# Row maxima subtracted as three bf16 parts in one pass; units of the gated stage in pairs on different rows; new orders of work

## The reference

```python
x = ln(x + L0_attn(x));  x = ln(x + L0_xattn(x, ctx)); x = ln(x + L0_ffn(x))
x = ln(x + L1_attn(x));  x = ln(x + L1_xattn(x, ctx)); x = ln(x + L1_ffn(x))
x = ln(x + L2_attn(x));  x = ln(x + L2_xattn(x, ctx, ctx)); x = ln(x + L2_ffn(x))
x = ln(x + L3_attn(x));  x = ln(x + L3_xattn(x, ctx, ctx)); x = ln(x + L3_ffn(x))
# softmax layers: exp(s - max(s)) / sum(exp(s - max(s)))
# L3_xattn, 8 heads of 16 features:
cs = cumsum(log_sigmoid(f)); log_D = where(tril, cs[:, None] - cs[None, :] + i[None, :], -inf)
D = exp(log_D - max(log_D)); C = (q @ k.T / sqrt(16)) * D
h = C / (maximum(abs(sum(C)), exp(-max(log_D))) + 1e-6) @ v
```

## Time and profile before

| | us |
|---|---|
| median of 3 runs | 1140.05 |
| lowest, highest | 1136.43, 1142.04 |
| profiled execution | 1138.05 |
| its span, first to last instruction | 1136.2 |
| PE busy | 979.7 (86%) |
| VectorE busy | 570.7 (50%) |
| ScalarE busy | 414.3 (36%) |
| mean granted clock of PE | 0.891 |

### The profile page before, as it was taken

How to read it: one execution, slowest core, us unless ns; L and a number is a source line. 1 busy time by engine, 2 the same in 40 slices (tenths; PEclk the granted TensorE clock), 3 DMA queues, 4 the chain that set the end, 5 groups by cost and what they waited for, 6 DMA issues and landing times. The chain is left out here.

```text
span 1136.2 us, 20415 instructions
## 1 busy us (share of the span) xinstructions
PE 979.7 (86%) x8329; PEld 710.0 (62%) x8329; DVE 570.7 (50%) x1585; ACT 414.3 (36%) x873; POOL 44.5 (4%) x68
## 2 busy tenths in 40 slices
PE   7689898999899879988697979999989898898781
PEld 4237776788787846745245757868878685674431
DVE  5733567452464653634624853655346464534326
ACT  2035323243545725623024234234354463331211
POOL 1200000000100000000000000001010000000000
PEclk9699999899999979959659999989999989997755
DMA  9000003000003011110000000121000300000000
GB/s 335 10 1 2 1 1 149 2 34 1 17 1 126 1 37 39 62 73 1 1 10 1 1 1 2 56 94 34 1 17 1 126 1 1 1 1 1 1 0 19
DMA packets 6830, 35.97 MB, mean 32 GB/s; under 512 B 722, under 2 KB 4306, under 8 KB 5459
## 3 DMA queue, kind: packets, MB, share of 16 engines
q1 hardware_dynamic: 6738, 34.68, 8.2%
HBM read 34.15 MB, written 0.52 MB: 31 GB/s over the span
## 5 line engine op out<-in xcount | busy, mean ns | idle before, releaser
L641 PE MATMUL bank<-xT,weights_F 128*128 128x256 f32 x832 | 203.4, 390 | 0.7 <-ACT p L1766 0.6
L641 PEld LDWEIGHTS bank<-xT,weights_F 128*128 128x128 f32 x832 | 155.1, 196 | 21.7 <-issue 1.7
L649 PEld LDWEIGHTS bank<-weights_F,p 128*128 128x128 f32 x1088 | 134.4, 192 | 18.4 <-issue 6.5
L649 PE MATMUL bank<-weights_F,p 128*128 128x128 f32 x1088 | 140.5, 277 | 2.5 <-DVE p L1322 2.5
L1694 ACT ACTIVATE p<-bank 128x512 f32<-128x512 f32 x160 | 84.3, 602 | 137.8 <-PE bank L487 119.0
L1306 DVE SCALAR_TENSOR_TENSOR res<-bank,comb,res 128x128 f32<-128x128 f32 x184 | 55.8, 345 | 68.6 <-PE bank L649 65.1
L1322 DVE TENSOR_TENSOR p<-p,bank 128x512 f32<-128x512 f32 x72 | 49.4, 686 | 65.1 <-PE bank L641 33.1
L1147 DVE TENSOR_REDUCE m_wide<-bank 128x4 f32<-128x512 f32 x96 | 60.7, 683 | 39.3 <-PE bank L748 32.5
L1766 ACT ACTIVATE p<-bank 128x512 f32<-128x512 f32 x72 | 42.5, 597 | 96.8 <-PE bank L641 96.3
L1842 ACT ACTIVATE p<-bank 128x512 f32<-128x512 f32 x64 | 36.8, 598 | 58.4 <-PE bank L641 58.3
L513 PE MATMUL bank<-p,vz 128*32 128x128 f32 x1280 | 44.2, 286 | 9.4 <-ACT p L1694 8.8
(11 more groups left out here) (323 smaller groups left out, 1524.9 us busy)
## 6 DMA issues: line engine op xcount, KB each, us to landing
weights_F<-in_L1f SPq DMA_DIRECT2D x2, 4096.0 KB, 13.2
weights_F<-in_L0f SPq DMA_DIRECT2D x2, 3456.0 KB, 12.9
weights_F<-in_L2f SPq DMA_DIRECT2D x2, 3456.0 KB, 12.1
weights_Y<-in_L1x_kv SPq DMA_DIRECT2D x2, 1024.0 KB, 10.1
weights_Z<-in_L1x SPq DMA_DIRECT2D x2, 1024.0 KB, 11.1
weights_Y<-in_L2a SPq DMA_DIRECT2D x2, 898.0 KB, 4.4
weights_Z<-in_L2x SPq DMA_DIRECT2D x2, 449.0 KB, 3.2
weights_L3m<-in_L3m SPq DMA_DIRECT2D x2, 288.0 KB, 5.8
```

Of the source, the lines that this page charges most:

```text
L641: m = mm(b[:, k * NT:(k + 1) * NT], W[weight][:, f:f + P], s.xT[:], start=True, stop=True)
L649: m = mm(b[:, tk(u)], h[:, tk(u)], w, start=k == 0, stop=k == len(chunks) - 1)
```

## The change

Four edits.

- Maxima. After the reductions VectorE splits each set of maxima into three bf16 parts that add up to the f32 value: copy to bf16, subtract, copy the rest to bf16, subtract again (`split_maxima`, four operations of 128x16 that wait for each other, with a yield between). The parts lie in columns 4k to 4k+3 of each 32 of `m_wide`, `pick` takes rows 0 to 11 of each 32, `m_diag` and the ones are bf16. `turn_maxima` waits for the last of these operations, where it waited for the last reduction.
- L3x. Units go in pairs (0, 3) and (1, 2), whose products lie on rows 0 to 63 and 64 to 127 and whose row sums lie on rows 0 to 31 and 32 to 63 (32 rows each instead of 8). A pair opens two banks for the products and then two for the sums; the order is both pairs, retrieved(0), retrieved(1). VectorE and ScalarE follow.
- `v17` has memory of its own. Two constants are made at the start, and `WARM`, a table for extra matmuls, is there but empty.
- All strings of `TURN_ORDER` are new, those of POOL and SP too.

```diff
-    put("pick", -(p[:, None] % 32 == np.arange(4)).astype(np.float32))
+    put("pick", -((p[:, None] % 32 < 12) & (p[:, None] % 4 == np.arange(4))).astype(np.float32))
...
+WARM = {"a": "", "b": ""}
...
-            self.m_diag = own("m_diag", NS, 4, T)
+            self.m_diag = sb(f"m_diag_{g}", [P, NS, 4, T], BF16)
+            self.m_part = sb(f"m_part_{g}", [P, 2, H], BF16)
+            self.v17 = own("v17", NS, HC, DC + 1)
...
                 def turn_maxima(st, u):
                     b = opened("dve", st, "mT", u)
-                    if st == "L0x":
-                        pe.wait_ge(*told("maxima"))
-                    else:
-                        pe.wait_ge(*freed(st, "s", u, 0, 3))
+                    pe.wait_ge(*told("maxima"))
...
-                        m = mm(heads(b[:], 4), const("ones")[rows32(i), 0:T], s.m_diag[rows32(i), u], start=first, stop=not first)
+                        m = mm(heads(b[:], 4), ones_bf[rows32(i)], s.m_diag[rows32(i), u], start=first, stop=not first)
...
+                    def units(first, second):
+
+                        both = (first, second)
+                        banks = [opened("dve", "L3x", "s", i) for i in both]
+                        for i, b in zip(both, banks):
+                            u, half = i // 2, i % 2
+                            filled(mm(heads(b[:], 4), s.ctxT[rows64(half), tk(u)], s.bd_c[rows64(half), u], start=True, stop=True),
+                                   "L3x", "s", i)
+                        banks = [opened("act", "L3x", "D", i) for i in both]
+                        for b in banks:
+                            mm(heads(b[:], 4), ident_bf[:], among(neg_causal_t_bf[:], 4), start=True, stop=False)
+                        for i, b in zip(both, banks):
+                            u, half = i // 2, i % 2
+                            filled(mm(heads(b[:], 4), const("ones")[rows32(u), 0:T], s.m_diag8[rows32(u), 4 * half:4 * half + 4],
+                                      start=False, stop=True), "L3x", "D", i)
...
-                    unit(0)
-                    yield
-                    unit(1)
+                    units(0, 3)
+                    yield
+                    units(1, 2)
                     yield
                     pe.wait_ge(*told("L3x_v17"))
                     pe.wait_ge(*told("L3x_ones"))
                     retrieved(0)
                     yield
-                    unit(2)
-                    yield
-                    unit(3)
-                    yield
                     retrieved(1)
...
+                def split_maxima(u):
+
+                    part = lambda k: heads(s.m_wide[:, u], 4)[:, :, 4 * k:4 * k + 4]
+                    done = o.count(dve.tensor_copy(heads(s.m_part[:, 0], 4), part(0)))
+                    yield
+                    dve.wait_ge(*done)
+                    done = o.count(dve.tensor_tensor(part(1), part(0), heads(s.m_part[:, 0], 4), ALU.subtract))
+                    yield
+                    dve.wait_ge(*done)
+                    done = o.count(dve.tensor_copy(heads(s.m_part[:, 1], 4), part(1)))
+                    yield
+                    dve.wait_ge(*done)
+                    o.count(dve.tensor_tensor(part(2), part(1), heads(s.m_part[:, 1], 4), ALU.subtract), sem("maxima"))
...
+            dve.memset(zeros_bf[:], 0.0).then_inc(S("masks"), 1)
             take_turns("dve", program)
...
-                    for i in range(4):
+                    for i in (0, 3, 1, 2):
...
-                            sp.wait_ge(*ring.full((pair, "L3x", "s", 3)))
+                            sp.wait_ge(*ring.full((pair, "L3x", "s", 2)))
```

More of the change, by code:

```diff
@@ L146 @@
     "pe":
[10 rows of a table removed]
-    "dve":
[9 rows of a table removed]
-    "act":
[7 rows of a table removed]
[10 rows of a table added]
+    "dve":
[9 rows of a table added]
+    "act":
[7 rows of a table added]
     "pool":
-        "a1 b1 a2 b2 a2 b2 a1 b1 a4 b1 a1 b2 a1 b2 a1 b1 a2 b1 a4 b6 a3 b3 a4 b1 a1 b2 a1 b2 a1 b2 a3 b3 ",
+        "a1 b1 a1 b2 a3 b1 a1 b1 a1 b1 a2 b1 a2 b2 a1 b2 a1 b1 a2 b1 a4 b4 a1 b2 a2 b2 a1 b1 a2 b1 a2 b2 a1 b2 a1 "
+        "b1 a2 b1 a1 b3 ",
     "sp":
-        "a3 b3 a18 b18 a23 b23 ",
+        "a3 b6 a18 b12 a23 b26 ",
 }
+WARM = {"a": "", "b": ""}
 def build(nc, dram, out):
@@ L219, in _build @@
     neg_causal_t_bf = sb("neg_causal_t_bf", [P, P], BF16)
+    ones_bf = sb("ones_bf", [P, P], BF16)
+    zeros_bf = sb("zeros_bf", [P, P], BF16)
     ones_row = const("ones")[0:1, 0:128]
@@ L330, in __init__ @@
             self.m_diag8 = self.p[0:64, 4:6].rearrange("p a (h t) -> p (a h) t", h=4)
-            self.v17 = self.m_diag[:].rearrange("p u j t -> p (u j t)")[:, 0:NS * HC * (DC + 1)] \
-                .rearrange("p (u h d) -> p u h d", u=NS, h=HC)
         def apart(self, u, block=0):
@@ L409, in _, with warm @@
             mm, tr = pe.matmul, pe.transpose
+            def warm(b, n):
+                for _ in range(n):
+                    mm(heads(b[:], 4), ident_bf[:], among(zeros_bf[:], 4), start=True, stop=True)
             def program(g):
@@ L413, in program @@
                 key = pair = turn = None
+                warmth = iter(WARM["ab"[g]].split())
                 def opened(by, *a):
-                    return ring.open((pair, *a), by)
+                    b = ring.open((pair, *a), by)
+                    warm(b, int(next(warmth, 0)))
+                    return b
                 def filled(ins, *a):
@@ L995, in L3x @@
                     yield
-                    def unit(i):
-                        u, half = i // 2, i % 2
-                        b = opened("dve", "L3x", "s", i)
-                        mm(heads(b[:], 4), s.ctxT[rows64(half), tk(u)], s.bd_c[rows64(half), u], start=True, stop=True) \
-                            .then_inc(ring.filled((pair, "L3x", "s", i)), 1)
-                        b = opened("act", "L3x", "D", i)
-                        mm(heads(b[:], 4), ident_bf[:], among(neg_causal_t_bf[:], 4), start=True, stop=False)
-                        filled(mm(heads(b[:], 4), const("ones")[32 * u:32 * u + 8, 0:T],
-                                  s.m_diag8[32 * u:32 * u + 8, 4 * half:4 * half + 4], start=False, stop=True), "L3x", "D", i)
+                    def units(first, second):
[12 more added lines that the diff above has]
+                                      start=False, stop=True), "L3x", "D", i)
                     def retrieved(u):
@@ L1063, in _ @@
             pe.wait_ge(*weights("con"))
-            pe.wait_ge(S("masks"), 3)
+            pe.wait_ge(S("masks"), 5)
             take_turns("pe", program)
@@ L1148, in maxima @@
                                 free(st, "s", u, 0, i))
+                    yield
+                    dve.wait_ge(*freed(st, "s", u, 0, 3))
+                    yield from split_maxima(u)
                 def block_maxima(st, u, blk):
@@ L1159, in block_maxima @@
                             dve.wait_ge(free(st, "s", u, k, 3), ring.freed((pair, st, "s", u, k, 3))[1])
-                        o.count(dve.tensor_tensor(heads(s.m_wide[:, u], 4)[:, :, 0:4], heads(s.mx[:, u, 0], 4),
-                                                  heads(s.mx[:, u, 1], 4), ALU.max), sem("maxima"))
+                        done = o.count(dve.tensor_tensor(heads(s.m_wide[:, u], 4)[:, :, 0:4], heads(s.mx[:, u, 0], 4),
+                                                         heads(s.mx[:, u, 1], 4), ALU.max))
+                        yield
+                        dve.wait_ge(*done)
+                        yield from split_maxima(u)
                 def pick_maxima(st, u):
@@ L1564, in keep @@
                         return o.count(dve.tensor_copy(held[u][:, 0:HC * 17], b[:, 0:HC * 17]), free("L3x", "o", u))
-                    unit(0)
-                    yield
-                    unit(1)
-                    yield
+                    for i in (0, 3, 1):
+                        unit(i)
+                        yield
                     keep(0)
@@ L1624, in _ @@
             dve.wait_ge(*weights("con"))
-            for dst, src in ((ident_bf, IDENT), (neg_causal_bf, const("neg_causal")), (neg_causal_t_bf, const("neg_causal_t"))):
+            for dst, src in ((ident_bf, IDENT), (neg_causal_bf, const("neg_causal")), (neg_causal_t_bf, const("neg_causal_t")),
+                             (ones_bf, const("ones"))):
                 dve.tensor_copy(dst[:], src).then_inc(S("masks"), 1)
+            dve.memset(zeros_bf[:], 0.0).then_inc(S("masks"), 1)
             take_turns("dve", program)
```

## The result

| | us |
|---|---|
| before, median of 4 runs | 1139.72 (1136.43 to 1142.04) |
| changed, median of 4 runs | 1110.05 (1103.07 to 1114.31) |
| ratio | 0.9732, 95% interval 0.9699 to 0.9765 |
| profiled execution of the changed kernel | 1112.03, span 1110.2 |
| granted clock, mean | 0.900 (before 0.891) |

The kernel became 29.7 us faster by the medians and 30.5 (3.8 either way) by the ratio, 2.7%. The forecast was 1105, the range 1082 to 1126.

What follows compares the result with a forecast made beforehand. TensorE, busy 979.7 of 1136.2 us, was taken as the bound, with waits in its queue left to lose. Gains of 25 and 18.7 less losses of 10 and 0.4 made 33 us off 1138.05: 1105, range 1082 to 1126.

Steps and rivals of the forecast that it cites:

- new orders: The newly laid out instruction orders of all engines: counted as zero, with 8 us either way.
- pairs in L3x: L3x units overlapped in pairs: 28 us of TensorE time go, new waits for banks take part, 18.7 us gained.
- split of the maxima: Four more VectorE operations before each of 32 transposes: 0.84 us delay each, partly covered, 10 us lost.
- subtraction in one pass: bf16 instead of f32 matmuls in 40 quartets: 33 us of TensorE time saved, three quarters passed on, 25 us.
- start: TensorE's first matmul waits for one more VectorE cast and a memset: 0.4 us lost.
- the last sign that I gave for a wrong forecast: The forecast is wrong if the clock differs from before over more than some 20 us.
- the missing quarter: Share of the 33 us saved on the subtraction not expected back, because TensorE then waits for ScalarE's exponentials.
- Rival (d): Longer waits ahead of the transposes drop the clock; slower, 1149 us if at 18 of 32 transposes; chance 0.06.
- The drain: Tiling mode change between mask and subtraction: at most 0.1 to 0.2 us a quartet; by the rule, sum 5 us worse.
- Rival (b): ScalarE's emptying of banks bounds: 10 of 25 us pass, 1120 us; sign: longer waits on exponentials; chance 0.14.
- Rival (c): The four bf16 subtraction matmuls run one after another: gain 3 us instead of 25, 1127 us; chance 0.07.
- rival (a): Pairing raises the clock in L3x, since pairs use more rows: 17 us more gained, 1088 us; chance 0.20.

## Why the prediction was right, and where it was off

The experiments make a chain from the kernel before to the changed one, each link the difference of two ratios:

| step | forecast, us | measured, us (95% interval) | half-clock time behind it, us |
|---|---|---|---|
| kernel before | | | 249 |
| new orders | 0 (8 either way) | -2.1 (1.6 either way) | 201 |
| pairs in L3x | -18.7 | -17.8 (2.9 either way) | 188 |
| split of the maxima | +10 | +8.9 (3.3 either way) | 188 |
| subtraction in one pass | -25 | -19.6 (4.4 either way) | 213 |
| start | +0.4 | not taken apart | |
| sum | -33 | -30.5 (3.8 either way) | |

The sum and each large term came near. But the last sign that I gave for a wrong forecast did appear: the half-clock time differs from before by 36 us, and I had set 20. PE is also busy 925 us and idle 185, where I had 915 and 160 to 175. So the number came out right although the clock was left out of it, and that is in part luck.

**What bounds the kernel** was read rightly for the two edits that take PE work away: about two thirds of it came back as run time. It doesn't hold for the orders, which took 13.3 us of busy time from PE and gave 2.1 back.

**The one pass.** The work was sized rightly: 0.32 us a quartet against my 0.28, 29.9 us of line 497 against 33. (The 17.9 us busy, where I had written 11, are records that overlap; 40 quartets of 0.32 are 13.) The wrong step was the pass-through. I laid the missing quarter on the emptying of the banks. PE's idle time hardly changed between the f32 and the bf16 kernel (183.1 and 185.2 us). What changed was the clock of the other matmuls: 25 us more at half clock and 10.4 us more of busy time, so that 29.9 less 10.4 less 2.1 of idle time leaves the 17.4 us by which the span shrank. Four pairs of kernels differ by the one pass:

| pair of kernels | worth of the one pass, us | half-clock time, us |
|---|---|---|
| with the split | 19.6 (4.4 either way) | 188 to 213 |
| without the split | 21.4 (3.3 either way) | 188 to 195 |
| old orders, no split | 19.1 (3.6 either way) | 250 to 258 |
| split, waits filled | 25.8 (5.6 either way) | 186 to 184 |

Half-clock time grows in three of them and not in the fourth, where the worth is largest. The intervals are too wide to say more. Rival (d) had this in part (a wait ahead of a transpose, then half speed), tied to longer waits. The waits for the maxima are longer with the one pass (12.1 us instead of 8.4), but the wait shown at 946.75 is the same 1.82 us in five of these kernels. It was followed by half clock in two (the changed one and the one without table loads) and by full clock in three (f32, sums over 8 rows, L3x one unit after the other). So what decides between the two levels behind a wait isn't shown. The additional half-clock time cost about 10 us, far from the 43 that it would have needed to turn the sign.

**The drain.** By the Trainium skill (TensorEngine Tiling (Array Packing), Tiling Modes, Key Properties) a change of tiling mode drains TensorE, and by that rule the sum would have been 5 us worse. The measured quartet, 0.32 us with the change of mode ahead of it and 0.24 for a lone mask, leaves 0.08 us for it, 3 us over 40 quartets (an estimate: four matmuls side by side may cost more than one anyway). No more of the rule than that shows here.

**Rival (b)**, the emptying of the banks, fell: in f32 the kernel was at 1127, not at 1120, and the waits for the exponentials are 22.6 us with the one pass and 23.5 without it. They had been 14.3 in the kernel before, so my sign for (b) did appear, but it came with the orders: with all work undone they are 22.5. **Rival (c)** fell with line 497 at 17.9 us instead of 38.

**The split.** 0.84 us a set and 10 us in all were right within 2 us. The way there was luck in part. I counted how much slack each transpose had in the old orders. The new orders left one wait of 0.9 us ahead of all transposes, where it had been 21.0, and with the split it is 8.4 us in f32 and 12.1 in bf16. My sign, waits of about 30 us, was wrong.

**The pairs.** The last L3x took 22.5 us for 23.2, with waits of 3.14 for 3.2 and 2.15 for 2.0. Two differences cancel in it: a wait of 1.08 us between the retrievals, which I didn't have, and retrievals of 3.0 and 3.6 us instead of 3.9, since the mean clock was 0.58 and not 0.50. For the others I took the clock as it was, which made six of all eight pairs slow. Three were at half clock (556.15, 1061.29 and 1069.47 in the trace). But without pairs, in the new orders, 9 of 16 units already ran at full clock, so this isn't rival (a) either, in which the pairs do it. PE lost 28.5 us of busy time by the pairing, as forecast. The 17 us of (a) don't follow from its terms: six pairs x 2.5 are 15, and the five retrievals that ran slow x 1.9 another 9.5, so that it stands for about 1080.

**The orders** gave 2 us where I had none, but not because nothing happened: less half-clock time and more waiting cancel. They also brought 24 table loads to ScalarE, 31 us of its time, whose cost can't be told from nothing. I read PE's side of the orders only.

## What to carry to other kernels

Here taking work from a busy TensorE left the work that stayed with more time at half clock, a third of the saving. Before passing a saving on, count how much of the run is at each level, and compare the whole run in several executions: a single stretch may be at full clock in one kernel and at half in the next with the same instructions and the same wait. Matmuls of zeros in the waits cost nothing that could be measured where they fit, and in the bf16 kernel they gave back 9 us (3 to 16). When units are overlapped by pairing, count the banks that a pair holds: the wait for the slower engines that free them can be read off before (3.2 us forecast, 3.14 measured). A new order of work that comes out at nothing can still move 13 us from busy to idle time, so measure it alone. And ask whether exactness is needed at all: a softmax doesn't change with its rounded maximum, which makes the whole split superfluous, 11 us.

## What the runs showed of the hardware

With the same orders, the subtractions in f32 gave 187 to 198 us at half clock and those in bf16 200 to 222, with PE idle alike. The same wait of 1.82 us, with the same transpose and scores behind it, was followed by full clock in the f32 kernel and in the bf16 kernel with sums over 8 rows, and by half clock in the changed kernel. Fillers in eleven waits lowered the half-clock time of the bf16 kernel to 173 to 192 us and left that of the f32 kernel at 185 to 189. Zero rows in a matmul made no difference that shows (8 or 32 rows; 2.3 us, 4.7 either way). Four bf16 matmuls of 512 columns on four 32-row strips hold PE for 0.32 us, four f32 ones for 1.08, and one bf16 matmul over all rows for 0.24. A load of a ScalarE table takes 1.28 us.
